# Relative-position rows with a padded pitch of 2,176 columns, and operand loads in groups of 48, 32 and 16 rows

## The reference

```python
        def _relative_shift(x):
            b, h, s, _ = x.shape
            x = jnp.pad(x, ((0, 0), (0, 0), (0, 0), (1, 0)))
            x = x.reshape(b, h, s + 1, s)
            return x[:, :, 1:, :].reshape(b, h, s, s)
        content_score = jnp.einsum('bhsp,bhtp->bhst', q + u, k)
        pos_score = jnp.einsum('bhsp,htp->bhst', q + v, pos)
        pos_score = _relative_shift(pos_score)
        score = (content_score + pos_score) / jnp.sqrt(jnp.float32(P))
        weights = jax.nn.softmax(score, axis=-1)
        out = jnp.einsum('bhst,bhtp->bhsp', weights, val)
```

## Time and profile before

| What | Value |
|---|---|
| Median of 3 runs | 10402.63 us (10396.37 to 10418.39) |
| The profiled execution's own time | 10403.32 us |
| Its span in the trace | 10401.5 us |
| Mean granted TensorE clock | 0.947 |
| PE busy | 8852.9 us (85%) |
| ACT busy | 5857.5 us (56%) |
| DVE busy | 5693.0 us (55%) |
| POOL busy | 2778.5 us (27%) |
| DMA queue of SP: bytes, share of 16 engines | 2459.12 MB, 63.6% |

### The profile page before, as it was taken

One profiled execution on the slowest core, in us unless ns is written; L12 is line 12 of the kernel. 1 busy time (PEld: TensorE's weight loads), 2 busy tenths in 40 slices (PEclk: granted clock), 3 DMA queues, 4 the chain that ended last, 5 costly groups with the idle time before them and its releaser, 6 DMA issues. The chain is left out here.

```text
span 10401.5 us, 254976 instructions
## 1 busy us (share of the span) xinstructions
PE 8852.9 (85%) x89696; PEld 5781.6 (56%) x89696; DVE 5693.0 (55%) x11468; ACT 5857.5 (56%) x10813; POOL 2778.5 (27%) x2893
## 2 busy tenths in 40 slices
PE   5888889899688888989968888898996888889899
PEld 2656666445466666644536556664553656666455
DVE  3655664564365566456436556545734655664673
ACT  3666665354366666445446666644544666664453
POOL 2333332100233333210023333321002333332101
PEclk7999999899899999989979999998997999999899
DMA  6999995110599999411069999932106999993210
GB/s 226 381 362 366 380 383 192 65 31 19 220 375 361 370 376 384 169 65 35 15 241 381 367 360 381 373 151 69 32 17 256 383 365 365 376 382 125 70 35 23
DMA packets 748142, 2476.58 MB, mean 238 GB/s; under 512 B 114080, under 2 KB 136096, under 8 KB 746528
## 3 DMA queue, kind: packets, MB, share of 16 engines
q1 hardware_dynamic: 746784, 2459.12, 63.6%
HBM read 1276.14 MB, written 1181.76 MB: 236 GB/s over the span
## 5 line engine op out<-in xcount | busy, mean ns | idle before, releaser
L695 DVE CUSTOM_DVE_ANT_0 z<-sc,z 128x1024 f32<-128x1024 f32 x2048 | 2495.5, 1219 | 1827.4 <-DMA z<-rel_rows 1564.1
L753 POOL TENSOR_SCALAR z<-z,nmax 128x1024 f32<-128x1024 f32 x2048 | 2270.9, 1120 | 4014.3 <-DVE nmax L705 4014.3
L668 ACT ACTIVATE pT<-rg 128x512 f32<-128x512 f32 x4096 | 2448.8, 598 | 744.9 <-PE rg L578 685.5
L578 PE MATMUL rg<-ident,z 128*128 128x128 f32 x16384 | 2536.1, 278 | 73.8 <-issue 66.2
L676 ACT ACTIVATE rel<-rg 128x512 f32<-128x512 f32 x3072 | 1721.0, 596 | 1377.0 <-PE rg L559 1370.8
L578 PEld LDWEIGHTS rg<-ident,z 128*128 128x128 f32 x16384 | 1998.9, 142 | 786.6 <-ACT rel L676 292.6
L559 PE MATMUL rg<-pos_s,qv_s 96*128 96x512 bf16 x4096 | 1593.1, 396 | 987.1 <-DVE rel L730 869.1
L989 ACT ACTIVATE pT<-rg 128x512 f32<-128x512 f32 (+3 forms) x2560 | 1226.0, 531 | 831.8 <-PE rg L921 497.9
L559 PEld LDWEIGHTS rg<-pos_s,qv_s 96*128 96x128 bf16 x4096 | 479.2, 118 | 1462.9 <-DVE rel L730 1117.1
L1005 DVE TENSOR_REDUCE mx_b<-sc 128x1 f32<-128x1024 f32 (+7 forms) x1024 | 1004.2, 990 | 514.1 <-PE sc L903 277.1
L599 PE MATMUL op<-pT,xnT 128*32 128x128 f32 x32768 | 1130.7, 280 | 0.0
(11 more groups left out here) (106 smaller groups left out, 7768.2 us busy)
## 6 DMA issues: line engine op xcount, KB each, us to landing
rel_rows<-rel SPq DMA_DIRECT2D x2048, 512.0 KB, 7.1
z<-rel_rows SPq DMA_DIRECT2D x2048, 512.0 KB, 7.0
v_heads<-rel SPq DMA_DIRECT2D x8, 4096.0 KB, 12.5
xnT<-v_heads SPq DMA_DIRECT2D x128, 256.0 KB, 3.3
qv_s<-qv_parts SPq DMA_DIRECT2D x384, 64.0 KB, 6.2
pos_s<-pos_parts SPq DMA_DIRECT2D x384, 64.0 KB, 7.2
xnT<-qu_parts SPq DMA_DIRECT2D x384, 64.0 KB, 6.3
z<-qu_parts SPq DMA_DIRECT2D x384, 64.0 KB, 2.1
```

The source lines that it names most:

```text
L578: mm = e.transpose(rg[:, T_BANK[q], (j - 4 * q) * P:(j - 4 * q + 1) * P], z[:, n % RING, j * P:(j + 1) * P], ident[:, :])
L668: e.activation(pT[:, t % 2, q * CH:(q + 1) * CH], rg[:, T_BANK[q], :], ACT.Exp, scale=SCALE).then_inc(p_ready[q], 1)
L695: e.tensor_tensor_reduce(out=zs, in0=scf[:, 2 * half * CH:2 * (half + 1) * CH], in1=zs, scale=1.0, scalar=-3.0e38, op0=ALU.add, op1=ALU.ma ...
L753: e.tensor_scalar(zs, zs, 1.0, nmax[:, n % 2:n % 2 + 1], ALU.mult, ALU.add).then_inc(AA[done], 1)
```

## The change

The rows in `rel_rows` get a pitch of W = 2,176 floats, and no zero is stored apart. Row i of a tile whose first row is i0 is now filled so that one read with a pitch of W - 1 from column 127 gives the shifted rows: up to column i0+127 of the written row the products are of row i with `pos` shifted (`edge` in `rows_of`), beyond it of row i+1 (the weights are `qv_s` moved by one column) with `pos`. The chunk in which this edge lies is made by two products (12 of 16 tiles; in the others the edge is a chunk's boundary). 128 more columns, the `tail`, come from one further product, `row_tail`, into the PSUM bank `op`; DVE copies them to `rel` after its copy of L737's kind. `pos_s` gets 16 columns ahead, zeroed once by POOL, which give the zero of the shift. The second written half has 1,152 columns in place of 1,024; a read needs only its own tile's write. `combine` now waits also for the tail's copy of the step before, since both use the bank `op`.

The operand loads become three pairs of 48, 32 and 16 rows (`GROUP`): the q side takes 3, 2 and 1 parts, the k side takes one part 3, 2 and 1 times. The bytes stay the same. They are issued in steps 1, 3, 5 and 8, 10, 12 of a head; attention B loads by the same function.

```diff
-FLAT = S * (S + 1)
+W = S + P
+PAD = 16
+FLAT = S * W
...
-QPART = [0, 1, 2, 0, 1, 0]
-KPART = [0, 0, 0, 1, 1, 2]
+GROUP = [(0, KROWS, 3), (1, 64, 2), (65, KROWS, 1)]
...
-                e.matmul(rg[:, R_BANK[c], :], qv_s[hd][:, i0:i0 + P], pos_s[hd][:, c * CH:(c + 1) * CH],
-                         start=True, stop=True).then_inc(r_full[c], 1)
+                edge = min(max(i0 + P - c * CH, 0), CH)
+                if edge > 0:
+                    j0 = PAD + S - P - i0 + c * CH
+                    mm = e.matmul(rg[:, R_BANK[c], 0:edge], qv_s[hd][:, i0:i0 + P], pos_b[hd][:, j0:j0 + edge],
+                                  start=True, stop=True)
+                if edge < CH:
+                    j0 = PAD + c * CH + edge - i0 - P - 1
+                    mm = e.matmul(rg[:, R_BANK[c], edge:CH], qv_s[hd][:, i0 + 1:i0 + P + 1],
+                                  pos_b[hd][:, j0:j0 + CH - edge], start=True, stop=True)
+                mm.then_inc(r_full[c], 1)
+
+            def row_tail(base, n, first):
+
+                hd, i0 = n // NT % NB, n % NT * P
+                if not first:
+                    e.wait_ge(tail_copied, base.tiles + n)
+                j0, m = PAD + S - i0 - P - 1, min(P, S - i0 - 1)
+                e.matmul(tail[0:m, :], qv_s[hd][:, i0 + 1:i0 + 1 + m], pos_b[hd][:, j0:j0 + P],
+                         start=True, stop=True).then_inc(tail_full, 1)
...
                 if here(s):
+                    e.wait_ge(tail_copied, base.tiles + (r if here(r - 1) else G))
                     combine(p, base, s)
...
                     rows_of(p, base, r, 1)
+                    row_tail(base, r, not began and r == 0)
                 if here(v):
                     values(p, base, v)
...
+                if here(r):
+                    e.wait_ge(tail_full, base.tiles + (r + 1))
+                    e.tensor_copy(rel[:, r % RING, S:W], tail).then_inc(tail_copied, 1)
...
+        def load_group(e, q, k, q_src, k_src, h, i, done):
+
+            first, last, reps = GROUP[i]
+            rows = slice(first, last, 2)
+            e.dma_start(q[rows, :], q_src[bass.ds(h, 1), 0:reps * HD, :].rearrange("a (r d) s -> (a d) r s", d=HD)
+                        ).then_inc(done, 16)
+            e.dma_start(k[rows, :], k_src[bass.ds(h, 1), i * HD:(i + 1) * HD, :]
+                        .rearrange("a (r d) s -> (a d) r s", d=HD).to_broadcast([HD, reps, S])).then_inc(done, 16)
...
-                if not last:
-                    e.wait_ge(rel_out[(n + 1) % RING], e.snap(moved(base, n + 1)))
-                    settle(e)
...
-                shifted = bass.AP(tensor=rel_d.tensor, offset=hd * FLAT + (i0 + 1) * S + c0, ap=[[S, P], [1, S // 2]])
+                shifted = bass.AP(tensor=rel_d.tensor, offset=hd * FLAT + i0 * W + P - 1 + c0, ap=[[W - 1, P], [1, S // 2]])
...
-                there = bass.AP(tensor=rel_d.tensor, offset=hd * FLAT + i0 * (S + 1) + 1 + c0, ap=[[S + 1, P], [1, S // 2]])
-                e.dma_start(there, rel[:, k, c0:c0 + S // 2]).then_inc(rel_out[k], 16)
+                if half:
+                    e.wait_ge(tail_copied, e.snap(base.tiles + (n + 1)))
+                    settle(e)
+                there = bass.AP(tensor=rel_d.tensor, offset=hd * FLAT + i0 * W + c0, ap=[[W, P], [1, c1 - c0]])
+                e.dma_start(there, rel[:, k, c0:c1]).then_inc(rel_out[k], 16)
...
-            for k in range(NB):
-                first = bass.AP(tensor=rel_d.tensor, offset=k * FLAT, ap=[[NT * (S + 1), P], [S + 1, NT], [1, 1]])
-                with nc.allow_non_contiguous_dma(reason="one zero ahead of each row"):
-                    e.dma_start(first, zero[:, :].rearrange("p (t o) -> p t o", o=1)).then_inc(zd, 16)
```

More of the change, by code:

```diff
@@ L123, in program @@
         qv_s = [sb("qv_s0", [KROWS, S], BF16), sb("qv_s1", [KROWS, S], BF16)]
-        pos_s = [sb("pos_s0", [KROWS, S], BF16), sb("pos_s1", [KROWS, S], BF16)]
+        pos_b = [sb("pos_s0", [KROWS, PAD + S], BF16), sb("pos_s1", [KROWS, PAD + S], BF16)]
+        pos_s = [t[:, PAD:PAD + S] for t in pos_b]
         k_sb = sb("k_sb", [KROWS, S], BF16)
-        rel = sb("rel", [P, RING, S])
+        rel = sb("rel", [P, RING, W])
         z = sb("z", [P, RING, S])
@@ L145, in program @@
         ident_b = sb("ident_b", [P, P], BF16)
-        zero = sb("zero", [P, NT])
         mx_b = sb("mx_b", [P, 2, NT])
@@ L189, in program @@
         po = op[:, 0:P]
+        tail = op[:, 2 * P:3 * P]
         on = op[:, P:P + OB * VW].rearrange("p (o w) -> p o w", o=OB)
@@ L255, in program @@
         qv_loaded = [sem("qv_loaded0"), sem("qv_loaded1")]
-        sem_zero = sem("spare_head_zero")
+        tail_full = sem("tail_full")
+        tail_copied = sem("tail_copied")
         PHASES = 9
@@ L260, in program @@
         LOADS = 17
-        QK_INC = 16 * 2 * len(QPART)
+        QK_INC = 16 * 2 * len(GROUP)
         def meet(e, b, k):
@@ L755, in pool_attn_a, with load_pair @@
             in_order(e, b, step)
[L757 to L766, removed]
+        def load_group(e, q, k, q_src, k_src, h, i, done):
[5 more added lines that the diff above has]
+                        .rearrange("a (r d) s -> (a d) r s", d=HD).to_broadcast([HD, reps, S])).then_inc(done, 16)
+        def load_pair(e, q, k, q_src, k_src, h, groups, done):
+            for i in groups:
+                load_group(e, q, k, q_src, k_src, h, i, done)
         def load_v(e, h, hd, done):
@@ L772, in sp_attn_a @@
         def sp_attn_a(e, b):
-            every = range(SLOTS)
+            every = range(len(GROUP))
             load_pair(e, qv_s[0], pos_s[0], qv_d, pos_d, 0, every, qv_loaded[0])
@@ L778, in sp_attn_a, with read_ready @@
             load_pair(e, qv_s[1], pos_s[1], qv_d, pos_d, 1, every, qv_loaded[1])
-            def read_ready(p, base, n, fresh, last):
+            def read_ready(p, base, n, fresh):
                 k = n % RING
@@ L788, in read_ready @@
                 settle(e)
-                if not last:
-                    e.wait_ge(rel_out[(n + 1) % RING], e.snap(moved(base, n + 1)))
-                    settle(e)
             def read_half(n, half):
                 k, hd, i0, c0 = n % RING, n // NT % NB, n % NT * P, half * S // 2
-                shifted = bass.AP(tensor=rel_d.tensor, offset=hd * FLAT + (i0 + 1) * S + c0, ap=[[S, P], [1, S // 2]])
+                shifted = bass.AP(tensor=rel_d.tensor, offset=hd * FLAT + i0 * W + P - 1 + c0, ap=[[W - 1, P], [1, S // 2]])
                 e.dma_start(z[:, k, c0:c0 + S // 2], shifted).then_inc(rel_in[k], 16)
             def write_half(base, n, half):
-                k, hd, i0, c0 = n % RING, n // NT % NB, n % NT * P, half * S // 2
+                k, hd, i0, c0, c1 = n % RING, n // NT % NB, n % NT * P, half * S // 2, (S // 2, W)[half]
                 for c in ((R_DVE, R_ACT[-1]) if half else (R_ACT[1],)):
@@ L811, in next_heads @@
                 nxt = (hd + 1) % NB
-                if at in range(1, 7) and not (final and hd + 1 >= HB):
+                if at in (1, 3, 5) and not (final and hd + 1 >= HB):
                     if at == 1:
@@ L821, in next_heads @@
                     load_v(e, e.snap(p * HB + (hd + 1)), nxt, AA[f"v_loaded{nxt}"])
-                if at in range(8, 14) and not (final and hd + 2 >= HB):
+                if at in (8, 10, 12) and not (final and hd + 2 >= HB):
                     if at == 8:
@@ L833, in step @@
                 if here(n):
-                    read_ready(p, base, n, s < 0 and n < RING, n % NT == NT - 1)
+                    read_ready(p, base, n, s < 0 and n < RING)
                 for half in range(2):
@@ L1089, in load_qk @@
             def load_qk(h, n):
-                load_pair(e, q_b[n % HB][0:KROWS, :], k_b[n % HB][0:KROWS, :], qu_d, k_d, h, range(SLOTS), BB[f"qk_loaded{n % HB}"])
+                load_pair(e, q_b[n % HB][0:KROWS, :], k_b[n % HB][0:KROWS, :], qu_d, k_d, h, range(len(GROUP)), BB[f"qk_loaded{n % HB}"])
             def max_rows(at, n):
@@ L1331, in _ @@
         def _(e):
-            e.memset(zero[:, :], 0.0).then_inc(zeroed, 1)
+            for t in pos_b:
+                e.memset(t[:, 0:PAD], 0.0).then_inc(zeroed, 1)
             e.wait_ge(loaded, 16 * LOADS)
```

7 lines of the change are left out of this document (2 added, 5 removed).

## The result

The changed kernel takes 10332.9 us (median; 10324.48 to 10338.86) against 10403.4 us: a ratio of 0.9929, 95% interval 0.9914 to 0.9943. It is 0.7% faster where 0.9% slower was forecast; 1 lies outside the interval. The profiled execution has 10338.86 us, its span 10337.1 us, 64.4 us shorter than before.

What follows compares the result with a forecast made beforehand. The prediction took DMA transfers to bound attention A and nothing else. It summed +157 - 48 - 15 = +94 us on 10403.3 us to 10497 us, slower by 0.9%, with a range from 10240 to 10640 us.

Steps and rivals of the forecast that it cites:

- What bounds the kernel: DMA transfers limit attention A and nothing else; added engine work is hidden up to about 0.71 us a tile, bytes never.
- More bytes written, +157 us: Attention A: the wider second half writes 64 KB more a tile, costing 157 us, with ends of 0 and 177 us.
- Fewer loads, -48 and -15 us: Earlier first write at attention A's four starts, -48 us; earlier first product at attention B's, -15 us; full stretch 0.
- PE, DVE, SP's wait for the tail, the read's wait, the zeros: Added engine work and changed waits in attention A, and no zeros stored ahead: each taken as 0.
- Aligned writes, unaligned reads, 0: In rel_rows the misalignment moves from writes to reads, taken as 0, with ends of -111 and +111 us.
- Rival 1: Alignment lifts attention A's rate to 395 GB/s, giving 10252 us; faster if the rate passes 385.2; chance 0.20.
- the quiet stretch: Early in a batch, few engines at work: the same transfer mix ran at 415 GB/s, 395 at a full share.
- Rival 2: Transfers are not the limit, added bytes are free and only the starts count: 10340 us; chance 0.08.
- The DVE wait: Sign: DVE's wait for the tile read back in attention A should stay near 1,600 us.

Runs made afterwards that it cites:

- e5_no_tail_bytes: Changed kernel with reads at the rows' pitch from column 0 (shift left out) and a second written half of 1,024 columns again: 10180.82 us, ratio 0.9781.
- e4_aligned_reads: Changed kernel with reads at a pitch of 2,176 columns from column 0, shift left out, so reads are aligned: 10339.43 us, ratio 0.9925.
- e6_no_tail_work: Changed kernel without the tail's product, its copy and the waits for both; stale values written, bytes unchanged: 10330.62 us, ratio 0.9923.
- the two experiments: Kernel before with the grouped loads alone, 10365.27 us, ratio 0.9953; changed kernel with the old 16-row loads, 10417.05 us, ratio 0.9998.
- e9_before_aligned: Kernel before with a pitch of 2,176 columns for writes and reads, both from column 0, shift left out: 10260.85 us, ratio 0.9858.
- e1_old_loads: Changed kernel with the 16-row loads of before, 24 a head: 10417.05 us, ratio 0.9998.
- e3_offset: Changed kernel with all rows in rel_rows moved by one float, 4 bytes, writes and reads alike: 10473.5 us, ratio 1.0053.
- e7_late_loads: Changed kernel with the second head's six position loads issued behind the writes of tiles 2, 3 and 4: 10331.39 us, ratio 0.9918.

## Why the prediction was wrong

**What bounds the kernel: right.** Bytes in attention A cost about what the transfers' rate says (e5_no_tail_bytes), and the tail's work on the engines costs nothing (e6_no_tail_work).

**More bytes written, +157 us: right.** 150 us by the ratios of e5_no_tail_bytes and e4_aligned_reads, and 151 us by their four stretches.

**Fewer loads, -48 and -15 us: right.** 11.5 and 3.7 us a batch at the two starts, 61 us; 49 and 69 us by the two experiments. That SP needs no longer for 48 rows was open, and holds at the start of the stage.

**PE, DVE, SP's wait for the tail, the read's wait, the zeros: right as a sum.** Only the tail's work with its waits was taken out by itself. The rest follows from three ratios: e9_before_aligned has 0.9858, the added bytes cost 0.0144, together 1.0002; e1_old_loads, which has besides these the split products, the tail's work, the unaligned reads and the changed waits, has 0.9998. So all of these together come to nothing, within some 25 us. The odd column offsets show no price: the full product takes 392 ns at an odd offset (L569) and at an even one (L565), where it was 390, and the tail's product takes 220 where I took 241.

**Aligned writes, unaligned reads, 0: this step failed.** I priced the fault at 3.7% of the writes, 111 us, and let the reads take back what the writes gained. Both halves were off. The gain of the write is 126 us on the changed kernel (e3_offset; 126 to 132 us over the four offsets), above my upper end, and 148 us on the kernel before, there with the new pitch in it (e9_before_aligned). That is 4.2 to 4.9% of the writes' half of the time, where I had 3.7% from stores that never filled the DMA engines. And the read takes back nothing (e4_aligned_reads). With the measured terms, 150 for the bytes, -61 to -69 for the loads and -126 to -148 for the writes in place of 0, the sum lies between -37 and -67 us; measured were -70.5, with an interval of about -59 to -90. So the aligned writes give the sign, and if they are worth only the 126, some 33 us stay unexplained.

What misled me was symmetry: with no row for an unaligned read I gave it the price of an unaligned write, and took the balance as the likeliest value with the doubt on both sides, where it should have been a rival with a chance of its own. The rule of the Trainium skill that I cited, from which I had estimated about 90 us for the reads, pointed the same way; e4_aligned_reads shows no such cost.

**The rivals.** Rival 1, alignment lifts the stage, is what happened, and the sign that I had given for it, a rate over 385 GB/s, came out: 387. As a test it is narrow, since the same rows gave windows of 385 in e1_old_loads and e7_late_loads. Its size was wrong: its 10252 us came from 395 GB/s, the rate of the quiet stretch, which was not reached, so not all that the stage falls short is due to alignment, and what the rest is stays open. Its reason, memory lines filled in part, is out for lines of up to 128 bytes. Rival 2 named 10340 us, 7 us from the result, with a mechanism that e5_no_tail_bytes refutes: the bytes cost 150 us and were paid by something else. A matching number was no proof.

The DVE wait, for which I had expected near 1,600 us as before, fell to 1294.4. As a sign it would have misled, since most of its fall is the added copy.

## What to carry to other kernels

Where transfers limit a stage, put the start of every row that is written to memory on a 256-byte boundary, and let the read have the odd offset if one side must. Here, with rows of 4,096 to 4,608 bytes, it was worth 126 us by itself, nearly as much as 6% more bytes in the writes cost (150 us). Count the transfers that are issued ahead of a stage's first real one: each cost about 0.64 us of SP's queue on the path, whether it brought 16 rows or 48. Where a price has no row in the trace, don't set it equal to its neighbour's and call the two cancelled: treat each as a case.

## What the runs showed of the hardware

- Writes of 4,096 to 4,608 bytes a row that start 4, 32, 64 or 128 bytes off a 256-byte boundary all lower the stage's rate from 387 GB/s to 375 or 376, at a share of 1.01 and 1.00; moved by 256 bytes, it is 386 again. Reads of 4,096 bytes show no such cost.
- With a second written half of 576 KB its median time from issue to landing is 7.8 us, and that of the first half, of 512 KB, is 6.2 us, where over both halves it had been 7.1 us.
- Splitting each 128-row write into two of 64 rows (four writes a tile, two of them narrower) lowered the rate at a full share from 383 to 353 GB/s, and SP's issues then filled about 580 of 700 us.
